# An S4-conditioned, quantized FFN on one core: a second copy of four kernels K, two buffers for the intermediate, and down's preparation over more passes

## The reference

```python
def cond(u, length, log_dt, C, log_A_real, A_imag, D):   # 32 heads, 64 states each
    mask = arange(512) < length[:, None]
    u_m = u * mask[:, None, :]
    dt = exp(log_dt); A = -exp(log_A_real) + 1j * A_imag; dtA = A * dt[:, None]
    Cs = C * (exp(dtA) - 1) / A
    K = 2 * einsum('hn,hnl->hl', Cs, exp(dtA[:, :, None] * arange(512))).real
    y = irfft(rfft(u_m, n=1024) * rfft(K, n=1024))[..., :512] + u_m * D[:, None]   # causal convolution
    return y * mask[:, None, :]

def ffn(x, w_gate, w_up, w_down, s_gate, s_up, s_down):   # 512 -> 1376 -> 512, ternary weights
    xq = int4_quant(x)                       # per row, scale by the mean of |x|
    gate, up = bitlinear(xq, w_gate, s_gate), bitlinear(xq, w_up, s_up)
    inter = int8_quant(up * square(relu(gate)))   # per row, scale by the max of |.|
    return bitlinear(inter, w_down, s_down)
# bitlinear: w_q = clip(round(w / (mean|w| + eps)), -1, 1), y = x @ w_q.T * mean|w| * s

out = x + ffn(cond(x, ...), ...)
```

## Time and profile before

| | |
|---|---|
| median of 3 runs | 201.41 us (201.2 to 201.56) |
| the profiled execution's own time | 201.68 us |
| its span, first to last instruction | 199.9 us |
| PE busy | 170.8 us (85%) |
| DVE busy | 156.1 us (78%) |
| ACT busy | 116.6 us (58%) |
| POOL busy | 27.4 us (14%) |
| chain that ended last: PE, DVE, DMA, issue | 62%, 17%, 9%, 5% |
| moved by DMA | 34.25 MB, mean 171 GB/s |

### The profile page before, as it was taken

How to read it: one execution, slowest core, us unless ns; L and a number is a source line. 1 busy time by engine, 2 the same in 40 slices (tenths; PEclk the granted TensorE clock), 3 DMA queues, 4 the chain that set the end, 5 groups by cost and what they waited for, 6 DMA issues and landing times.

```text
span 199.9 us, 3333 instructions
## 1 busy us (share of the span) xinstructions
PE 170.8 (85%) x1062; PEld 90.8 (45%) x1077; DVE 156.1 (78%) x411; ACT 116.6 (58%) x195; POOL 27.4 (14%) x71
## 2 busy tenths in 40 slices
PE   1002897999999679999999999999999999999992
PEld 1002865555554334545454545454545444444461
DVE  6998997466598988986898978787878798887951
ACT  2466987366999596863548282828272736334520
POOL 5023998970000000000000000000000000000000
PEclk9999999999999999999999999999999999999999
DMA  4999495999879989999646465545452524435244
GB/s 120 383 369 329 115 271 189 202 313 389 187 169 210 242 179 232 189 241 181 150 132 130 132 137 147 118 146 115 146 116 43 110 48 103 93 87 117 60 108 105
DMA packets 48913, 34.25 MB, mean 171 GB/s; under 512 B 37024, under 2 KB 37312, under 8 KB 48896
## 3 DMA queue, kind: packets, MB, share of 16 engines
q1 hardware_dynamic: 45008, 25.91, 57.0%
q10 hardware_dynamic: 3888, 8.13, 12.9%
HBM read 21.07 MB, written 4.28 MB: 127 GB/s over the span
## 4 chain that ended last, share of the span: by engine, by line
PE 62%; DVE 17%; DMA 9%; issue 5%; ACT 5%; DVEq 0%; ACTq 0%
PE down_ps L662 13%; PE gate_ps L624 13%; PE up_ps L629 12%; PE tr_dve_ps L551 6%; PE conv_ps L551 6%; PE conv_ps L662 5%; DMA it_int<-inter_q 5%; DMA raw<-in_L_ffn_w_down_dram 4%; PE tr_act_ps L537 2%; DVE int L1045 2%; ACT g L798 2%; DVE inter L1150 2%; PE gate_ps L675 1%; DVE y L1073 1%; PE down_ps L551 1%
## 5 line engine op out<-in xcount | busy, mean ns | idle before, releaser
L798 ACT ACTIVATE g<-gate_ps,gu_scale 128x416 f32<-128x416 f32 (+2 forms) x48 | 30.4, 634 | 43.5 <-PE gate_ps L624 43.5
L1150 DVE SCALAR_TENSOR_TENSOR inter<-up_ps,gu_scale,g 128x416 f32<-128x416 f32 (+2 forms) x48 | 33.3, 693 | 22.3 <-ACT g L801 22.0
L629 PE MATMUL up_ps<-up_t,q_t 128*128 128x512 bf16 (+2 forms) x190 | 44.6, 357 | 2.2 <-DVE inter L1150 2.1
L624 PE MATMUL gate_ps<-gate_t,q_t 128*128 128x416 bf16 (+2 forms) x180 | 42.6, 356 | 0.6
L801 ACT ACTIVATE g<-g 128x416 f32<-128x416 f32 (+2 forms) x48 | 28.1, 586 | 1.5
L1158 DVE TENSOR_REDUCE imax<-inter 128x1 f32<-128x928 f32 (+1 forms) x32 | 27.8, 870 | 1.1
L629 PEld LDWEIGHTS up_ps<-up_t,q_t 128*128 128x128 bf16 x192 | 18.5, 98 | 21.3 <-DVE inter L1150 3.4
L662 PE MATMUL down_ps<-down_t,i_t 128*128 128x512 bf16 (+1 forms) x121 | 27.9, 379 | 0.0
L624 PEld LDWEIGHTS gate_ps<-gate_t,q_t 128*128 128x128 bf16 x192 | 17.5, 98 | 15.7 <-issue 2.2
L725 ACT ACTIVATE int<-raw 128x2048 bf16<-128x2048 f32 (+3 forms) x8 | 15.6, 1945 | 8.8 <-DMA raw<-in_L_ffn_w_gate_dram 5.2
L551 PE MATMUL conv_ps<-toep,x_t 128*64 128x512 f32 (+3 forms) x128 | 19.0, 439 | 1.5 <-ACT x_t L753 1.0
(11 more groups left out here) (187 smaller groups left out, 200.6 us busy)
## 6 DMA issues: line engine op xcount, KB each, us to landing
toep<-k_back SPq DMA_DIRECT2D x16, 512.0 KB, 5.1
out_dram<-o_sb SPq DMA_DIRECT2D x30, 128.0 KB, 2.4
raw<-in_x_dram ACTq DMA_DIRECT2D x3, 512.0 KB, 5.8
raw<-in_x_dram SPq DMA_DIRECT2D x3, 512.0 KB, 8.7
raw<-in_L_ffn_w_down_dram ACTq DMA_DIRECT2D x1, 1472.0 KB, 12.4
raw<-in_L_ffn_w_down_dram ACTq DMA_DIRECT2D x1, 1280.0 KB, 9.0
raw<-in_L_ffn_w_gate_dram ACTq DMA_DIRECT2D x1, 1024.0 KB, 5.8
raw<-in_L_ffn_w_gate_dram SPq DMA_DIRECT2D x1, 1024.0 KB, 10.5
```

The lines of the kernel that those rows point to most:

```text
L624: mm = pe.matmul(gate_ps[bank][:, 0:cn], q_t[m % 3][:, i, :], gate_t[:, i, c0:c0 + cn], start=(i == 0), stop=(i == KB - 1))
L629: mm = pe.matmul(up_ps[bank][:, 0:cn], q_t[m % 3][:, i, :], up_t[:, i, c0:c0 + cn], start=(i == 0), stop=(i == KB - 1))
L798: nc.scalar.activation(g2[bank][:, 0:cn], gate_ps[bank][:, 0:cn], ACT.Relu, scale=gu_scale[m % 4][:, 0:1]).then_inc(relu_done, 1)
L1150: v.scalar_tensor_tensor(out=inter[:, c0:c0 + cn], in0=up_ps[bank][:, 0:cn], scalar=gu_scale[m % 4][:, 1:2], in1=g2[bank][:, 0:cn], op0=AL ...
```

## The change

Three things change.

K's parts 0 and 1, the first four tiles, are stored twice, to `k_back` and to a new array `k_twin`. The Toeplitz tiles 0 to 3 are loaded by two DMAs of 64 partitions each: the even partitions from `k_back`, the odd ones from `k_twin`. The later tiles are loaded as before.

`inter_q` becomes two buffers, used in turn by even and odd passes. VectorE waits in pass m for the turn of pass m - 2.

Down's steps are spread: one quarter each is rounded by VectorE and by ScalarE in pass 2 and again in pass 3; SP turns quarters 0 and 2 in pass 3, 1 and 3 in pass 4; VectorE copies quarter 0 in pass 4 and 1 in pass 5, ScalarE copies 2 in pass 4 and 3 in pass 5. The half loads of x move from passes 1 and 4 to passes 2 and 6.

```diff
+    k_twin = nc.dram_tensor("k_twin", [KH, 2 * JR, JB], F32, kind="Internal")
...
-        inter_q = sb("inter_q", [P, IB * P], I16)
+        inter_q = [sb(f"inter_q{p}", [P, IB * P], I16) for p in range(2)]
...
                 sp.dma_start(dst, k_sb[:, h0:h1, :]).then_inc(k_stored[i], 16)
+                if h1 <= KH:
+                    twin = k_twin.ap()[h0:h1].rearrange("h a b -> a h b")
+                    sp.dma_start(twin, k_sb[:, h0:h1, :]).then_inc(k_stored[i], 16)
 
             def load_toep(n):
+                if n < KH:
+                    sp.wait_ge(k_stored[k_part(n)], 32)
+                    for odd, store in enumerate((k_back, k_twin)):
+                        src = bass.AP(store, n * 2 * (L + P) + odd, [[2, P // 2], [L + P, 2], [1, L]])
+                        sp.dma_start(toep[n % 4][odd:P:2], src).then_inc(toep_loaded[n % 4], 16)
+                    return
...
-                if m in (2, 3):
-                    turn_down(2 * m - 4)
-                    turn_down(2 * m - 3)
-                if m in (1, 4):
-                    load_half(sp, 3 if m == 1 else 4, 0)
+                if m in (3, 4):
+                    turn_down(m - 3)
+                    turn_down(m - 1)
+                if m in (2, 6):
+                    load_half(sp, 3 if m == 2 else 4, 0)
...
-                pe.wait_ge(toep_loaded[n % 4], 16 * (n // 4 + 1))
+                pe.wait_ge(toep_loaded[n % 4], 16 * (n // 4 + 2))
...
                 elif m < T - 2:
+                    if m == 5:
+                        down_copy(3)
                     y_sum(m + 2)
                 relu_square(1)
...
                 relu_square(2)
-                if m in (3, 4):
-                    down_copy(2 * m - 5)
+                if m == 4:
+                    down_copy(2)
                 if m == 0:
                     y_round(2)
-                if m == 4:
+                if m == 6:
                     for i in range(2):
                         act.wait_ge(w_rounded[2][i], rounds(2, i))
                     load_half(act, 4, 1)
...
-                if m == 1:
+                if m == 2:
                     load_half(act, 3, 1)
-                if m == 2:
-                    down_round(2)
-                    down_round(3)
+                if m in (2, 3):
+                    down_round(m)
...
-            v.memset(inter_q[:, I:IB * P], 0)
+            for p in range(2):
+                v.memset(inter_q[p][:, I:IB * P], 0)
...
-                if m in (3, 4):
-                    down_copy(2 * m - 6)
+                if m in (4, 5):
+                    down_copy(m - 4)
...
-                    down_round(0)
-                    down_round(1)
+                if m in (2, 3):
+                    down_round(m - 2)
...
-                if m >= 1:
-                    dve.wait_ge(it_loaded[(m - 1) % IRING], 16 * ((m - 1) // IRING + 1))
+                if m >= 2:
+                    dve.wait_ge(it_loaded[(m - 2) % IRING], 16 * ((m - 2) // IRING + 1))
```

More of the change, by code:

```diff
@@ L434, in _ @@
                     wait(sp, it_copied, m - IRING)
-                    sp.dma_start_transpose(it_int[(m - 1) % IRING], inter_q[:]
+                    sp.dma_start_transpose(it_int[(m - 1) % IRING], inter_q[(m - 1) % 2][:]
                                            ).then_inc(it_loaded[(m - 1) % IRING], 16)
@@ L636, in turn_last @@
                     mm = pe.transpose(tr_act_ps[:, c * P // 2:(c + 1) * P // 2].bitcast(BF16),
-                                      inter_q[:, c * P:(c + 1) * P].bitcast(BF16), ident_bf[:])
+                                      inter_q[(T - 1) % 2][:, c * P:(c + 1) * P].bitcast(BF16), ident_bf[:])
                 mm.then_inc(it_turned, 1)
@@ L643, in turn_last @@
                     mm = pe.transpose(tr_dve_ps[0:r, o:o + P // 2].bitcast(BF16),
-                                      inter_q[:, c * P:c * P + r].bitcast(BF16), ident_bf[:])
+                                      inter_q[(T - 1) % 2][:, c * P:c * P + r].bitcast(BF16), ident_bf[:])
                 mm.then_inc(it_turned, 1)
@@ L847, in _ @@
             act.wait_ge(iscale_ready, 1)
-            nc.scalar.activation(inter_q[:, IT_SPLIT * P:I], inter[:, IT_SPLIT * P:I], ACT.Copy,
+            nc.scalar.activation(inter_q[(T - 1) % 2][:, IT_SPLIT * P:I], inter[:, IT_SPLIT * P:I], ACT.Copy,
                                  scale=iscale[:]).then_inc(last_quant, 1)
@@ L1195, in _ @@
                 step(v.tensor_scalar(gam127[:], gamma[:], EPS, 1.0 / 127.0, ALU.add, ALU.mult))
-                if m >= 1:
-                    dve.wait_ge(it_loaded[(m - 1) % IRING], 16 * ((m - 1) // IRING + 1))
+                if m >= 2:
+                    dve.wait_ge(it_loaded[(m - 2) % IRING], 16 * ((m - 2) // IRING + 1))
                 if m < T - 1:
                     step(v.reciprocal(iscale[:], gam127[:]))
-                    v.tensor_scalar(inter_q[:, 0:I], inter[:], iscale[:], None, ALU.mult).then_inc(inter_quant, 1)
+                    v.tensor_scalar(inter_q[m % 2][:, 0:I], inter[:], iscale[:], None, ALU.mult).then_inc(inter_quant, 1)
                 else:
@@ L1203, in _ @@
                     dve.wait_ge(iscale_ready, 1)
-                    v.tensor_scalar(inter_q[:, 0:IT_SPLIT * P], inter[:, 0:IT_SPLIT * P], iscale[:], None,
+                    v.tensor_scalar(inter_q[m % 2][:, 0:IT_SPLIT * P], inter[:, 0:IT_SPLIT * P], iscale[:], None,
                                     ALU.mult).then_inc(inter_quant, 1)
```

## The result

The changed kernel takes 210.63 us (median of 4 runs, 209.94 to 211.9), the kernel before 201.31 beside it (201.13 to 201.56): ratio 1.047, 95% interval 1.042 to 1.052. A second set of six runs, on another chip, gave 1.040 (1.033 to 1.046). A ratio leaves out the runs that lie over 1.5% above the fastest of their kernel, so it need not be the quotient of the medians given, which are of all runs. The profiled execution after took 210.41 us, its span is 208.6, 8.7 more than the 199.9 of before.

The account below looks back on a forecast made before the run. TensorE, full from 104 us on, was taken as the bound, so earlier delays stay. 201.68 - 1.17 + 6.89 (waits at down) + 1.7 (clock) + 0.1 (twin) = 209.2, 208.9 against the median; 209.0 said, range 203.2 to 211.5.

Parts of the forecast that it names:

- Passes 2 and 3: Rounding of down's weights spread over these passes: VectorE's tail of pass 2 ends sooner, shifting the start of pass 5 by -1.17 us.
- 1.2 us sooner than 72.00: Sign in the profile after: convolution 6 starts about 1.2 us before the 72.00 us of the kernel before.
- ScalarE's wait for quarter 3: Pass 5: ScalarE stands still 4.8 us until the transpose of down's quarter 3 lands at 88.3 us.
- The hole: TensorE ahead of the first down product: waits 7.5 us for VectorE's copy of quarter 1, ready at 94.4 us.
- 6 to 8.5 us, ended by VectorE's copy of quarter 1: Sign in the profile after: TensorE without work that long right ahead of the first down product, until that copy.
- The clock: TensorE behind the hole: runs slowly for some 4.2 us after its rest, costing 1.7 us (0 to 3.3).
- Rival A2: Ahead of and behind the first down product: same stall, but the clock holds; 207.5 us, chance 0.2.
- The twin: Start of the kernel: later landing of tile 0 costs at most 0.35 us; 0.1 taken, second memset of inter_q included.
- B: Pass 5: quarter 3 lands before ScalarE asks for it; convolution 9 +1.4 us, time 203.2 us, chance 0.1.
- C: Passes 2 to 4 give back more than 1.17 us, up to 3.63; faster, 200.7 us, chance 0.06.

## Why the prediction was right, and where its sizes were off

209.0 was said, 210.63 came. The mechanism was the one predicted, step by step:

- **Passes 2 and 3**: 1.17 us said, 1.09 came; the wait of the up product shows it directly (0.54 us instead of 1.64). The 0.28 us in it that was put down to the second inter_q is not that buffer's: the spread with one buffer has the same 0.54. But convolution 6 was not 1.2 us sooner than 72.00: it came at 72.71 in the first profile, since 1.81 us had been lost ahead of it, and at 71.22 in the second.
- **ScalarE's wait for quarter 3**: 4.8 said, 4.29 and 4.36 came. Behind the turn of y the transpose took 89.75 - 81.65 = 8.1 us instead of 8.6: down's transposes landed 4.6 to 4.9 us after their issue, where 5.3 had been taken from pass 3 of the kernel before. Why they were quicker is not shown.
- **The hole**: 7.5 said, 6.99 and 7.07 came, with the half us of the line above. The sign "6 to 8.5 us, ended by VectorE's copy of quarter 1" was there.
- **The clock**: 1.7 said; 1.60 in the first profile (3.98 - 2.38), 1.8 when the hole is filled. The size is in part luck. It was 4.2 us (the two rows lie 25.50 - 21.19 = 4.31 apart) at 0.62 / 1.03 = 0.60 of the speed; here some 3 us of the work ran at the lower level, 1.2 GHz, from 95.81 to about 98.8, as the granted clock of the stretches of 2 us shows. Rival A2 leaned on a column that reads 1.00 throughout before; here the column itself shows 0.79. What was taken from the slow transposes of the earlier trace rows, that TensorE is slow behind a rest, held.
- **The twin**: 0.1 was taken and "at most 0.35" said, from 0.9 us of later landing. In the first profile the load came 27.67 - 26.52 = 1.15 us later, and 0.62 of it reached VectorE's mask: the bound was passed there. It had left out SP's issue, 0.6 to 0.7 us for a half against 0.45 for a whole tile. But how much of the 0.62 is the twin's is not shown, since that mask starts between 29.45 and 30.26 in the profiles of kernels with neither twin nor halves. The twin alone measured +0.9 us (0.1 to 1.7).
- **What was not in the sum**: that the landing of down's weights scatters (their sum starts between 47.16 and 49.71 us over all profiles), and that before itself scatters with its clock. In the second profile, in which that landing is close to before's, the span is 207.5, or 7.6 more than before, against 7.5 predicted. So close an agreement is luck: that execution was the fastest of its six, on another chip, and by the ratio the loss there is 8.1 us (0.0397 x 203.23).

Rivals B and C needed quarter 3 in time. The experiment with the early transposes shows that even then about 4 us of hole stay. B's +1.4 was too low: with the transposes nearly in time (1.34 us of wait) the kernel was still 2.5% slower, because the hole that is left is 4.05 us long and also costs the clock (4.85 and 2.95 us for the products and the convolution behind it, instead of 2.54 and 2.37).

## What to carry to other kernels

Work that is spread over more passes to smooth one of them has to be checked at its consumer, not where it is done: the last copy sets the start, and a copy that stands in a strict queue behind a transfer holds up all that is behind it. Before moving work later, look for an engine that waits earlier: here ScalarE's 2.12 us in pass 3 took a rounding, and the convolution of that pass came only 0.20 us later. And a hole on TensorE can cost more than its length, since the work behind it runs slower: filling one with work without a use gained 1.8 us here.

## What the runs showed of the hardware that was not expected

- Holes of the same length did not cost the same: behind 4.08 us of hole the down products took 3.93 us and the convolution 2.38, behind 4.05 us 4.85 and 2.95, and behind 7.07 us 4.32 and 2.37. These are single profiles.
- The clock can fall in holes that are short, and need not: with the buffers alone it fell behind waits of 1.20 and 0.97 us, and the convolution took 4.01 us instead of 2.37; with one buffer and early copies behind 2.22 and 0.88 us (4.54 us). In the profile of before, with 1.64 and 0.97 us, it held. With waits of 0.31 to 0.55 and about 1 us it held in every profile here.
- Four half loads took SP 2.64 us to issue, two whole ones of the same bytes 0.90. From the issue of the first half to the landing of the second it took some 3.9 us, and 4.0 for a whole tile.
